# One block for attention and gates, with the gates' buffers placed in attention's memory and their inputs loaded during its last heads

## What is computed

```python
node_support = node_adj_norm @ h
edge_output = _gru_cell(node_support, h, edge_Wih, edge_Whh, edge_bih, edge_bhh)
edge_support = _gat_head(h, node_adj_norm, edge_adj_norm, gat_W[0], gat_a[0])   # 3 heads are summed
...
edge_support = edge_support / HEADS
node_output = _gru_cell(edge_support, h, node_Wih, node_Whh, node_bih, node_bhh)
return de[:, None] * edge_output + dn[:, None] * node_output
```

## Time and profile before

| what | value |
|---|---|
| three timed runs | 2696.13, 2703.39, 2705.26 us; median 2703.39 |
| profiled execution | 2697.63 us, of which the span of the trace is 2695.8 us |
| PE busy in the span | 86% |
| DVE busy in the span | 80% |
| ACT busy in the span | 40% |
| attention's last PE instruction ends | at 2579.15 us |
| first gate product starts | at 2590.45 us |

### The profile page before, as it was taken

The page is one execution under the profiler, slowest core; times in us unless marked ns, Lnnn a source line. Parts: engine busy times, 40 slices in busy tenths (PEclk is TensorE's granted clock), DMA queues, the critical chain, the costliest instruction groups (busy, mean ns, idle before and its releaser), DMA issues. The chain is left out here.

```text
span 2695.8 us, 53797 instructions
## 1 busy us (share of the span) xinstructions
PE 2329.1 (86%) x17795; PEld 1969.8 (73%) x17795; DVE 2159.1 (80%) x6687; ACT 1069.1 (40%) x1803; POOL 152.2 (6%) x342
## 2 busy tenths in 40 slices
PE   7999999879889978889967369987999999999985
PEld 2666666657777867767757368976999999999942
DVE  4777777578787888888889677758999999999836
ACT  5666666434334434334421220014444334443323
POOL 0000000101111110010000100000000000000000
PEclk8999999989999989999978779999999999999987
DMA  3000000022223312222202225551333433334220
GB/s 133 2 1 1 1 1 1 1 102 93 88 103 113 118 52 103 103 95 94 103 18 102 108 101 211 210 190 52 132 128 117 140 103 133 124 122 135 79 90 26
DMA packets 57310, 244.88 MB, mean 91 GB/s; under 512 B 6929, under 2 KB 18576, under 8 KB 43344
## 3 DMA queue, kind: packets, MB, share of 16 engines
q1 hardware_dynamic: 57040, 241.99, 25.7%
HBM read 235.15 MB, written 6.82 MB: 90 GB/s over the span
## 5 line engine op out<-in xcount | busy, mean ns | idle before, releaser
L2103 PE MATMUL a_acc<-H,pT 128*128 128x128 f32 x4056 | 547.8, 277 | 11.6 <-ACT a_rows L2135 3.8
L2103 PEld LDWEIGHTS a_acc<-H,pT 128*128 128x128 f32 x4056 | 495.3, 192 | 28.6 <-DVE pT L2237 19.9
L991 PE MATMUL small<-XR,wT 128*128 128x128 f32 x2756 | 378.2, 283 | 27.5 <-ACT wT L1261 26.8
L991 PEld LDWEIGHTS small<-XR,wT 128*128 128x128 f32 x2756 | 343.8, 197 | 43.3 <-ACT wT L1261 43.3
L862 PE MATMUL lg<-kT,qs 128*128 128x512 f32 (+1 forms) x742 | 339.1, 593 | 27.0 <-ACT e L1179 16.8
L72 DVE MAX8 cand<-e 128x8 f32<-128x64 f32 (+3 forms) x1898 | 302.9, 241 | 47.5 <-issue 24.6
L2237 DVE TENSOR_TENSOR pT<-a_tr,a_adjT 128x512 f32<-128x512 f32 (+1 forms) x546 | 316.7, 645 | 20.7 <-PE a_tr L2062 15.6
L2062 PE MATMUL a_tr<-ident,prob 128*128 128x128 f32 x2028 | 311.3, 274 | 10.9 <-ACTq L2129 10.9
L1261 ACT ACTIVATE wT<-tr 128x512 f32<-128x512 f32 (+1 forms) x371 | 206.3, 566 | 274.6 <-PE tr L981 273.6
L891 PE MATMUL accR<-XR,adj 128*128 128x129 f32 x2704 | 314.0, 276 | 0.0
L891 PEld LDWEIGHTS accR<-XR,adj 128*128 128x128 f32 x2704 | 309.9, 193 | 0.0
(11 more groups left out here) (351 smaller groups left out, 2423.8 us busy)
## 6 DMA issues: line engine op xcount, KB each, us to landing
adj<-in_adjT SPq DMA_DIRECT2D x52, 1664.0 KB, 7.2
g_adj<-in_adjT SPq DMA_DIRECT2D x26, 1664.0 KB, 7.0
a_adj<-in_adj SPq DMA_DIRECT2D x26, 1664.0 KB, 6.9
a_adjT<-in_adjT SPq DMA_DIRECT2D x156, 256.0 KB, 3.9
a_adjT<-in_adjT SPq DMA_DIRECT2D x26, 128.0 KB, 4.3
XT<-in_x_t SPq DMA_DIRECT2D x1, 1664.0 KB, 7.2
hT_scratch<-hT SPq DMA_DIRECT2D x1, 1664.0 KB, 11.1
nsT_scratch<-nsT SPq DMA_DIRECT2D x1, 1664.0 KB, 5.3
```

What stands on the lines that cost most here:

```text
L991: mm = eng.matmul(accA[:, :], wT[(k * NC + c - 1) % 2][:, o:o + P], xa[:, j, 0:P], start=(j == 0), stop=(j == T - 1))
L2103: mm = eng.matmul(acc[:, :], pT[g % RING][:, (j % 4) * P:(j % 4 + 1) * P], H[:, j, :], start=(j == 0), stop=(j == T - 1))
```

## The change

`attention` becomes `attention_and_gates`; `gates_and_output` no longer opens a block and no longer allocates. It makes five functions, which attention's block calls at the end of its five engines' streams. The tensors of the gates are views: state, the two supports, the transposed output and the squares lie in rows 0 to 4 of `EB`, the weights, biases and statistics in row 5, and `r`, `z`, `arg`, `s`, `mix` and `edge` in the three `prob` tiles. The eight PSUM banks are attention's six `a_tr` banks, the bank of `a_acc` and a bank `a_small` (before: `a_rs`), in which the turned rows and the projection lie. SP issues 28 of the 29 loads before the stores of the last two tiles, after a wait for the last `logits`; the attention support of the last chunk follows those stores. Two waits are new on PE and SP: the z product of unit 1, whose bank is `a_small`, waits until ACT has copied the last projection; SP waits for the stores of tiles 0 to 23 before it loads the first piece of `gsT`.

```diff
-def attention(nc, d, dims, H, ident, epm, negs):
+def gates_and_output(ctx, nc, d, dims, H, ident, diag, room, probs, banks, gs_stored, sup_copied):
...
+    free = [room[:, room.shape[1] - 1, :]] + probs
...
+    hT = room[:, 0, :]
+    support = [room[:, 1 + g, :] for g in range(2)]
+    OT = room[:, 3, :]
...
+    r, z, arg, s = ([sb(n, f"o_{name}{i}", [P, CH]) for i in range(2)]
+                    for name, n in (("r", 1), ("z", 1), ("arg", 2), ("s", 2)))
...
+    sums = [banks[0:4], [banks[4], banks[7], banks[5], banks[6]]]
...
+    def early_loads(eng):
...
+        for c in range(NC):
+            eng.dma_start(hT[:, cols(c)], d["hT"][:, cols(c)]).then_inc(chunk_loaded[c], 16)
+            eng.dma_start(support[0][:, cols(c)], d["nsT"][:, cols(c)]).then_inc(chunk_loaded[c], 16)
+            if c == 0:
+                for k in range(2):
+                    eng.wait_ge(gs_stored[k], 16 * (T // 2))
+            if c < NC - 1:
+                eng.dma_start(support[1][:, cols(c)], d["gsT"][:, cols(c)]).then_inc(chunk_loaded[c], 16)
+
+    def late_load_and_stores(eng):
+        for k in range(2):
+            eng.wait_ge(gs_stored[k], 16 * (T // 2 + 1))
+        eng.dma_start(support[1][:, cols(NC - 1)], d["gsT"][:, cols(NC - 1)]).then_inc(chunk_loaded[NC - 1], 16)
...
+            if u == 1:
+                eng.wait_ge(sup_copied, T)
...
-        acc = ps("a_acc", [P, P])
-        rs = ps("a_rs", [P, 2, P])
-        rt, sup = rs[:, 0, :], rs[:, 1, :]
+        acc_bank, small_bank = ps("a_acc", [P, 512]), ps("a_small", [P, 512])
+        acc, rt, sup = acc_bank[:, 0:P], small_bank[:, 0:P], small_bank[:, P:2 * P]
...
                 after(PAIRS - 1, 0, False, True)
+                eng.wait_ge(logit_ready, seq(PAIRS, 0))
+                early_loads(eng)
                 store(PAIRS - 1, 0)
                 store(PAIRS - 1, 1)
-                for k in range(2):
-                    eng.wait_ge(gs_stored[k], 16 * (PAIRS + 1))
+                late_load_and_stores(eng)
...
                 project(PAIRS - 1, len(order) - 1)
+                products(eng)
```

More of the change, by code:

```diff
@@ L1 @@
+import math
 from contextlib import ExitStack
@@ L1919, in attention, with attention_and_gates @@
+def attention_and_gates(nc, d, dims, H, ident, diag, epm, negs):
     N, NP, T = dims
@@ L1971, in attention @@
         gs_stored = [sem(f"a_gs_stored{i}") for i in range(2)]
+        early_loads, late_load_and_stores, products, gates, blends = gates_and_output(
+            ctx, nc, d, dims, H, ident, diag, EB, [t[:, :] for t in prob], tr + [acc_bank, small_bank], gs_stored, sup_copied)
         EB_GROUPS = 2 * HEADS * NC
@@ L2166, in _ @@
                 copy_turned(PAIRS - 1, len(order) - 1)
+                gates(eng)
             @block.vector
@@ L2255, in _ @@
                 over_pairs(eng, pair)
[L2258 to L2382, removed]
-                    eng.drain()
-                    eng.sem_inc(squared, 1)
-                eng.wait_ge(var_ready, 1)
-                eng.activation(var[:, :], var[:, :], ACT.Sqrt).then_inc(std_ready, 1)
-            @block.vector
-            def _(eng):
-                eng.wait_ge(weights, 16 * 8)
-                for g in range(2):
-                    eng.tensor_tensor(b_rz[g][:, :], b_in[g][:, 0:2], b_h[g][:, 0:2], ALU.add)
-                    eng.tensor_scalar(b_new[g][:, :], b_in[g][:, 2:3], 2.0, None, ALU.mult)
-                eng.drain()
-                eng.sem_inc(biases_ready, 1)
-                def candidate(u):
-                    c, g, i = u // 2, u % 2, u % 2
-                    n = width(c)
-                    rp, zp, inp, hnp = sums[i]
-                    eng.wait_ge(r_ready, u + 1)
-                    eng.scalar_tensor_tensor(arg[i][:, 0:n], hnp[:, 0:n], b_h[g][:, 2:3], r[i][:, 0:n],
-                                             ALU.add, ALU.mult)
-                    eng.drain()
-                    eng.wait_ge(in_summed, u + 1)
-                    eng.tensor_tensor(arg[i][:, 0:n], arg[i][:, 0:n], inp[:, 0:n], ALU.add).then_inc(arg_ready, 1)
-                def blend(u):
-                    c, g, i = u // 2, u % 2, u % 2
-                    n = width(c)
-                    eng.wait_ge(s_ready, u + 1)
-                    eng.wait_ge(z_ready, u + 1)
-                    eng.scalar_tensor_tensor(mix[:, 0:n], s[i][:, 0:n], -2.0, hT[:, cols(c)], ALU.mult, ALU.add)
-                    eng.drain()
-                    eng.scalar_tensor_tensor(mix[:, 0:n], mix[:, 0:n], 1.0, z[i][:, 0:n], ALU.add, ALU.mult)
-                    eng.drain()
-                    if g == 0:
-                        eng.scalar_tensor_tensor(edge[:, 0:n], s[i][:, 0:n], 2.0, mix[:, 0:n], ALU.mult, ALU.add)
-                    else:
-                        eng.scalar_tensor_tensor(mix[:, 0:n], s[i][:, 0:n], 2.0, mix[:, 0:n], ALU.mult, ALU.add)
-                        eng.drain()
-                        eng.scalar_tensor_tensor(OT[:, cols(c)], mix[:, 0:n], -2.0, edge[:, 0:n], ALU.add, ALU.add)
-                    eng.drain()
-                    eng.sem_inc(mixed, 1)
-                candidate(0)
-                for u in range(1, UNITS):
-                    candidate(u)
-                    blend(u - 1)
-                blend(UNITS - 1)
-                for c in range(NC):
-                    own = slice(tiles(c)[0], tiles(c)[-1] + 1)
-                    eng.wait_ge(turned, c + 1)
-                    for t in tiles(c):
-                        eng.scalar_tensor_tensor(H[:, t, :], rows_bank(c)[:, (t % 4) * P:(t % 4 + 1) * P],
-                                                 diag[:, t:t + 1], H[:, t, :], ALU.mult, ALU.add,
-                                                 accum_out=total[:, t:t + 1])
-                    eng.drain()
-                    eng.tensor_scalar(negmean[:, own], total[:, own], -1.0 / P, None, ALU.mult)
-                    eng.drain()
-                    eng.sem_inc(mean_ready, 1)
-                eng.wait_ge(squared, NC)
-                eng.tensor_scalar(var[:, :], var[:, :], 1.0 / P, EPS, ALU.mult, ALU.add).then_inc(var_ready, 1)
-                eng.wait_ge(std_ready, 1)
-                eng.reciprocal(rstd[:, :], var[:, :])
-                eng.drain()
-                for t in range(T):
-                    eng.tensor_scalar(H[:, t, :], H[:, t, :], negmean[:, t:t + 1], rstd[:, t:t + 1],
-                                      ALU.add, ALU.mult)
-                    if t in (HALF - 1, T - 1):
-                        eng.drain()
-                        eng.sem_inc(normed, 1)
@@ L2455, in program @@
+                blends(eng)
 def program(nc, d, dims):
@@ L2465, in program @@
         normalize_and_sum(nc, d, dims, H, ident, diag, epm, negs)
-        attention(nc, d, dims, H, ident, epm, negs)
-        gates_and_output(nc, d, dims, H, ident, diag)
+        attention_and_gates(nc, d, dims, H, ident, diag, epm, negs)
 def kernel(x, adj, L0_gnn_W1, L0_gnn_W2, L0_gnn_W3, L0_gnn_U1, L0_gnn_U2, L0_gnn_ln_g, L0_gnn_ln_b,
```

170 lines of the change are left out of this document (added).

## The result

| | before | after |
|---|---|---|
| median of 6 runs each | 2702.18 us | 2688.70 us |
| lowest and highest | 2696.13, 2705.26 | 2681.91, 2691.66 |
| profiled execution | 2697.63 us | 2681.91 us |
| its span | 2695.8 us | 2680.1 us |

The ratio of after to before is 0.9943 with a 95% interval of 0.9927 to 0.9959: 15.4 us less, 11 to 20. 2686.5 us were forecast, in a range of 2680 to 2696, and a gain of 13.96.

The account below looks back on a forecast made before the run. PE bounds the kernel, with an 11.30 us hole waiting for gate loads. Closing it plus 2.66 us of clock gives 13.96 us; 2700.5 - 14.0 = 2686.5 us, range 2680 to 2696.

Parts of the forecast that it names:

- The hole closes: PE's wait for loads between attention's last projection and the first gate product disappears: 11.30 us gained.
- The clock stays up: PE starts the gates' unit 0 at full clock, its first three products taking 2.59 us, not 5.25: 2.66 us gained.
- What follows is unchanged: From unit 0's fourth product to the end, the remaining 100.1 us shift as a whole.
- The queues: SP issues 28 loads by 2563.2, the late load lands at 2591.3, and the reordered stores and new waits cost nothing.
- Disturbance: Loads beside attention's last heads slow PE by 0, at most 0.4 us; rival 1.5 us, 2688, chance 0.81 with the forecast.
- Half clock at the start: Rival at the gates' first products: PE starts at half clock, only 11.3 us gained, 2689.2 us; chance 0.07.
- The late piece: Rival: all `gsT` pieces go out only after tile 25's store lands; gain 4.8 us, 2695.7 us; chance 0.05.
- Starved fetch: Rival in attention's last pair and first gate products: PE's instruction fetch queues behind loads, two stalls 30 us, 2716.5; chance 0.04.
- A sign of being wrong that did show: The prediction is wrong if a difference stands in a stage ahead of attention's last pair; no size given.
- The level: Whole-kernel time before the change, taken as 2700.5 us, the middle of three timed runs and the profiled one.

Follow-up runs that it names:

- Late loads: The change, but SP issues the 28 loads behind the stores of tiles 24 and 25, still in one block; profiled execution 2700.69 us.
- two blocks: The change, but with the gates' streams in a block of their own behind attention's, loads still early; run twice, profiled executions 2691.23 and 2692.18 us.
- the faster end: The change plus the last normalisation shared by DVE and ACT, the second run with 16 to 10 tiles and earlier table load; ratios to before 0.9947 and 0.9933.
- the repeat: The change once more, unedited, for a second trace; profiled execution 2684.40 us.

## Why the prediction was right, step by step

- **The hole closes: right.** 11.30 us were counted, 11.47 came, since the first product even overlaps the end of the projection. The table splits it: early loads alone take the stand from 11.30 to 2.56, the merged block takes the remaining 2.7. Neither part closes the hole by itself, and the merged block alone takes 1.3 off it.
- **The clock stays up: right in its size, for a reason only half seen, and with some luck.** 2.66 us were counted and 2.67 came (5.25 - 2.58), but both numbers lean on one trace of before. Late loads, with nearly as long a stand, lost only 4.25 - 2.58 = 1.67, so in other executions of before this term may be some 1 us smaller; there is only one trace of that kernel, so this was not measured. I had priced the clock as something that goes with a long hole. The runs with two blocks show that 2.56 us of standing lose it too, for 1.6 and 2.6 us. So with the loads early, the second half of the change, the merged block, is worth 7.69 - 2.41 = 5.3 or 6.72 - 2.41 = 4.3 us, not the 2.7 of its stand.
- **What follows is unchanged: right.** 100.06 against 100.10.
- **The queues: right.** 28 loads took 14.9 us to issue (14.6 by the sum), the new waits of PE and SP don't show, and the late load, bounded at 2591.3, was issued at 2579.59, 60 us ahead of its use.
- **Disturbance: 0, as taken**, up to 397 GB/s.
- **The rivals.** Half clock at the start didn't happen in any of the six traces with early loads in one block, the two with the faster end included; PE had not stood still. What I had set against it, that the clock outlasted these waits and two us of idleness, was weak: in the first trace with two blocks it fell within 1 us of the same projection. The late piece: PE's first product waits for no load. Starved fetch: not seen even with 8.9 MB.
- **A sign of being wrong that did show.** I had named a difference in a stage ahead of attention's last pair. There is one, 1.5 us, but the repeat has -1.0 in its place, and attention itself is the same to 0.02 us. As a sign it was badly chosen, since those stages differ by more than that from one execution to the next.
- **The level.** The forecast was laid at 2700.5 - 14.0. The median of before over six runs is 2702.18, so 1.7 of the 2.2 us by which 2686.5 missed 2688.70 is the level of before, not the change. By the medians the gain is 13.5 us, by the ratio 15.4, by the seam 14.14; the first two carry the spread of the stages ahead. That 2686.5 came within 2.2 us of the median of six such runs is partly luck.

## What to carry to other kernels

Where one stage ends on a busy PE and the next begins with loads, move the loads into the tail of the first stage and merge the two in one block, for which buffers must be found in memory that the first has finished with. Do both: with the early loads alone PE still stands through the last store and the engines' meeting, and in both traces it paid for that short stand again in its clock. Judge such an edit by the stretch that it touches in the trace, when whole runs of the kernel spread as widely as the gain.

## What the runs showed of the hardware that was not expected

The clock granted to PE fell 2.85 us or more after PE stopped in the kernel before, 2.45 us or more after with late loads, over 2 us after in one trace with two blocks and within 1 us in the other, after the very same instructions. A stand of 2.56 us therefore cost 1.6 us in one trace and 2.6 in the next, one of 10.04 us cost 1.7, one of 11.30 us cost 2.7, and stands of 0.84 and 1.76 us cost nothing in the one trace that each has. The Trainium skill, "TensorE: Matmul & The Clock Gate", Part 1, says that the moment of the change varies between runs since the chip's watch isn't started by the kernel; these traces agree for the fall, and the page tells of it for the rise only.
